# The last stage's TensorE program as a loop: rounds of sixteen tiles with fixed addresses, and a small ring for the split state

## What is computed

```python
def _L3_conv_ref(x, weight, idx_a, idx_b):
    cross = x[..., idx_a] * x[..., idx_b]
    feat = jnp.concatenate([x, x * x, cross], axis=-1)
    return jnp.einsum('bcij,cijo->bcio', feat, weight)
...
x = x + _L3_conv_ref(_gn(x), L3_conv_weight, L3_conv_idx_a, L3_conv_idx_b)
```

## Time and profile before

| | |
|---|---|
| median of 3 runs | 1283.17 us (1258.48 to 1284.13) |
| profiled execution | 1278.0 us, its span 1276.2 us, granted TensorE clock 0.677 |
| busy, share of the span | DVE 56%, PE 48%, ACT 40%, POOL 16% |
| last stage | first gather 835.8 us, last output issued 1273.8 us |
| queues | q1 (SP) 236.02 MB, q0 (POOL) 8.92 MB, q8 (instructions) 1.79 MB |
| chain that ended last | PE 31%, issue 24%, DMA 21%, DVE 18% of the span |

### The profile page before, as it was taken

How to read it: one execution, slowest core, us unless ns; L and a number is a source line. 1 busy time by engine, 2 the same in 40 slices (tenths; PEclk the granted TensorE clock), 3 DMA queues, 4 the chain that set the end, 5 groups by cost and what they waited for, 6 DMA issues and landing times.

```text
span 1276.2 us, 46246 instructions
## 1 busy us (share of the span) xinstructions
PE 607.6 (48%) x20656; PEld 484.3 (38%) x20656; DVE 713.7 (56%) x877; ACT 507.9 (40%) x716; POOL 204.3 (16%) x241
## 2 busy tenths in 40 slices
PE   2122121242699999412112122256675755556666
PEld 2112121232698989412112111034343433434344
DVE  6886565698543544796645659733453443334344
ACT  5575656570000000366555546132342333233333
POOL 1021111100111121021112110051303122121200
PEclk9555555566898989755555555687677577778777
DMA  9699999922999999789999991055657477464651
GB/s 274 157 280 226 226 230 230 237 68 59 234 235 234 231 227 240 180 230 232 212 214 218 215 309 38 8 165 172 201 187 219 159 228 218 162 201 148 217 164 55
DMA packets 50961, 246.90 MB, mean 193 GB/s; under 512 B 10992, under 2 KB 23280, under 8 KB 30256
## 3 DMA queue, kind: packets, MB, share of 16 engines
q1 hardware_dynamic: 46496, 236.02, 71.1%
q0 software_dynamic: 4336, 8.92, 2.5%
HBM read 219.20 MB, written 17.32 MB: 185 GB/s over the span
## 4 chain that ended last, share of the span: by engine, by line
PE 31%; issue 24%; DMA 21%; DVE 18%; ACT 3%; SPq 2%; POOL 1%; DVEq 0%; POOLq 0%; ACTq 0%
DMA work<-image 18%; PE psum L861 10%; PE psum L932 7%; PE psum L899 6%; PE psum L915 5%; PE psum L849 3%; DVE stats L573 2%; DVE state_b L780 2%; ACT state_b L526 2%; DMA image<-work 2%; DMA wring<-in_w 1%; DVE work L625 1%; DVE state_a L740 1%; DVE stats L744 1%; DVE state_a L618 1%
## 5 line engine op out<-in xcount | busy, mean ns | idle before, releaser
L780 DVE TENSOR_TENSOR state_b<-psum,state_b 128x512 f32<-128x512 f32 x256 | 163.8, 686 | 265.8 <-ACT state_b L526 264.6
L526 ACT ACTIVATE state_b<-psum 128x512 f32<-128x512 f32 x256 | 141.0, 596 | 292.1 <-PE psum L899 287.1
L849 PE MATMUL psum<-work,signs 96*32 96x64 f16 x6144 | 91.4, 241 | 347.8 <-DMA work<-image 307.6
L849 PEld LDWEIGHTS psum<-work,signs 96*32 96x32 f16 x6144 | 84.5, 129 | 354.8 <-issue 335.3
L861 PE MATMUL psum<-work,wring 96*128 96x128 f32 x1536 | 185.0, 285 | 37.4 <-DMA work<-image 37.4
L861 PEld LDWEIGHTS psum<-work,wring 96*128 96x128 f32 x1536 | 182.8, 201 | 39.7 <-issue 36.7
L408 ACT ACTIVATE signs<-wring 96x3072 f16<-96x3072 f32 x64 | 175.7, 2747 | 7.6 <-DMA wring<-in_w 7.6
L932 PE MATMUL psum<-state_b,wring 128*32 128x32 f32 x8192 | 125.8, 217 | 64.6 <-issue 64.1
L932 PEld LDWEIGHTS psum<-state_b,wring 128*32 128x32 f32 x8192 | 104.5, 128 | 135.6 <-issue 120.3
L682 DVE TENSOR_REDUCE abs_sums<-wring 96x2432 f32 x56 | 149.8, 2674 | 1.1
L899 PE MATMUL psum<-work,sel 64*128 64x512 f16 x512 | 108.4, 484 | 36.5 <-DMA work<-signs 17.4
(11 more groups left out here) (129 smaller groups left out, 615.9 us busy)
## 6 DMA issues: line engine op xcount, KB each, us to landing
wring<-in_w SPq DMA_DIRECT2D x96, 1152.0 KB, 16.0
wring<-in_pairs SPq DMA_DIRECT2D x64, 1024.0 KB, 5.7
work<-image SPq DMA_DIRECT2D x99, 272.0 KB, 10.7
image<-work SPq DMA_DIRECT2D x98, 128.0 KB, 4.3
work<-signs POOLq DMA_DIRECT2D x128, 64.0 KB, 5.8
state_a<-in_x SPq DMA_DIRECT2D x8, 512.0 KB, 8.6
work<-in_own SPq DMA_DIRECT2D x8, 512.0 KB, 6.5
out<-state_a SPq DMA_DIRECT2D x16, 256.0 KB, 6.0
```

Source lines behind the costliest of these rows:

```text
L526: act.activation(left[:, n % LSLOTS, :], psum[:, 2 * (n % 3), :], ACT.Copy, scale=1.0 / HALF_SCALE / HALF_SCALE).then_inc(left_made, 1)
L780: dve.tensor_tensor(feats[:, n % FSLOTS, :], psum[:, 2 * (n % 3) + 1, :], left[:, n % LSLOTS, :], ALU.mult).then_inc(feats_made, 1)
L849: last = pe.matmul(psum[g * C:(g + 1) * C, s, v * cols:(v + 1) * cols], wt[:, v, g, t, :], win[:, g * V + v + t, :], start=(v == 0 and t = ...
```

## The change

PE's last stage becomes a loop of 15 rounds, one group each, with a 16th group unrolled behind it. [...]

- `wpairs` has 4 slots instead of 6, one for each step of a group; `feats` 8 instead of 6.
- All parts of the split state lie in `parts` (each part has its own place and semaphore). POOL copies the columns of step k into slot k % 4 of a new `ring` (`copy_ring`), out of which PE gathers.
- `own_w` holds one group (256 KB and 4 x 32 KB) in one slot, and is loaded for each group; POOL copies the group's `xn` into `own_x` (`copy_own`), ACT squares it into `own_xsq`.
- `spread` moves from POOL's queue to SP's, after every eighth step.
- Own terms come in two halves, at tiles 0 and 8; a result is a half group (256 columns), added and written 32 times instead of 16.
- Gather t + 2 now waits for ACT's copy of tile t (`left_made`); the two factors use 2 and 4 banks. The mix of tile t follows each gather.
- Waits on PE compare with numbers worked out in registers.

Before, the 16 spread transfers of a part stood in POOL's queue and the own weights once a part. The diff, cut:

```diff
@@ -58,10 +58,15 @@
-WSLOTS = 6
+WSLOTS = 4
 WSTEP = PT * POS * W
-OWN = C * W
-FSLOTS = 6
+HALF = GROUP // 2
+GT = GROUP * PT
+GCOLS = GROUP * C4 * B
+OWN = GROUP * C4 * W
+ASLOTS = 2
+BSLOTS = 4
+FSLOTS = 8
...
-        xn = work[:, 0:2 * PART].rearrange("p (s n) -> p s n", s=2)
-        xsq = work[:, 2 * PART:4 * PART].rearrange("p (s n) -> p s n", s=2)
-        parts = work[:, 4 * PART:8 * PART].bitcast(F16).rearrange("p (s g n) -> p s g n", s=2, g=G)
-        own_w = work[:, STATE:STATE + 4 * OWN].rearrange("p (s k n) -> p s k n", s=2, k=2)
+        parts = work.bitcast(F16).rearrange("p (g n) -> p g n", g=G)
...
+        own_w = beside[:, 0:2 * OWN].rearrange("p (k n) -> p k n", k=2)
+        own_x, own_xsq = (beside[:, 2 * OWN + k * GCOLS:2 * OWN + (k + 1) * GCOLS] for k in range(2))
         hi_lo = signs.rearrange("p s n -> p (s n)")[:, 0:4 * PART].rearrange("p (s k n) -> p s k n", s=2, k=2)
+        ring = signs.rearrange("p s n -> p (s n)")[:, 4 * PART:4 * PART + GROUP * FCOL].rearrange("p (s n) -> p s n", s=GROUP)
...
+            load_own(0)
+            def spread(i):
+                sp.wait_ge(hi_split, i + 1)
+                sp.wait_ge(lo_split, i + 1)
+                for k in range(2):
+                    for g in range(G):
+                        for side in range(2):
+                            first = (2 * side + k) * W
+                            sp.dma_start(parts[first:first + W, g, i * PART:(i + 1) * PART],
+                                         hi_lo[g * W:(g + 1) * W, i % 2, k, :]).then_inc(parts_in[i], 16)
             for i in range(2):
-                load_own(i)
+                spread(i)
             for k in range(NK):
                 sp.wait_ge(mixed, PT * (k + 1))
                 if k + WSLOTS < NK:
                     load_pairs(k + WSLOTS)
-                if k % KPART == 1 and 2 <= k // KPART + 1 < V:
-                    sp.wait_ge(own_used, k // KPART * (KPART // GROUP))
-                    load_own(k // KPART + 1)
-                if k % GROUP == 1 and k > GROUP:
-                    sp.wait_ge(result_made, k // GROUP)
-                    cols = slice((k // GROUP - 1) * GROUP * C4 * B, k // GROUP * GROUP * C4 * B)
+                grp, half = k // GROUP, k % GROUP // HALF
+                if k % GROUP == 1 and grp + 1 < NGROUP:
+                    sp.wait_ge(own_used, 2 * (grp + 1))
+                    load_own(grp + 1)
+                if k % (2 * GROUP) == 2 * GROUP - 1 and (grp + 3) // 2 < V:
+                    spread((grp + 3) // 2)
+                if k % HALF == 1 and k > HALF:
...
+            def copy_ring(k):
+                if k % (2 * GROUP) == 0:
+                    pool.wait_ge(parts_in[k // GROUP // 2], 16 * 4 * G)
+                if k >= GROUP:
+                    pool.wait_ge(gathered, (k - GROUP + 1) * PT)
+                pool.tensor_copy(ring[:, k % GROUP, :].rearrange("p (g n) -> p g n", g=G),
+                                 parts[:, :, k * C4 * B:(k + 1) * C4 * B]).then_inc(ring_made, 1)
+            def copy_own(grp):
+                pool.wait_ge(xn_made[3], grp // 2 + 1)
+                if grp:
+                    pool.wait_ge(own_used, 2 * grp)
+                pool.tensor_copy(own_x, xn[:, grp // 2 % 2, grp % 2 * GCOLS:(grp % 2 + 1) * GCOLS]).then_inc(own_copied, 1)
+            m_op, r_op = (t[:, 0:B].unsqueeze(1).to_broadcast([P, C, B]) for t in (mean, rstd))
...
+            normalise(1)
+            for grp in range(NGROUP):
+                copy_ring(grp * GROUP)
+                copy_ring(grp * GROUP + 1)
+                copy_own(grp)
+                if grp % 2 and grp // 2 + 2 < V:
+                    normalise(grp // 2 + 2)
+                copy_ring(grp * GROUP + 2)
+                copy_ring(grp * GROUP + 3)
         CONSTS = 16 * 5
...
+            def gather(j, t):
+                if t % PT == 0:
+                    pe.wait_ge(ring_made, j * GROUP + (t // PT + 1))
                 for side in range(2):
                     half = slice(side * 2 * W, (side + 1) * 2 * W)
-                    last = pe.matmul(psum[:, 2 * (n % 3) + side, :], sel[half, t * P:(t + 1) * P],
-                                     parts[half, i % 2, :, cq * C4 * B:(cq + 1) * C4 * B], start=True, stop=True)
+                    bank = (0, ASLOTS)[side] + t % (ASLOTS, BSLOTS)[side]
+                    last = pe.matmul(psum[:, bank, :], sel[half, t % PT * P:(t % PT + 1) * P],
+                                     ring[half, t // PT, :], start=True, stop=True)
                 last.then_inc(gathered, 1)
-            def own_terms(grp):
-                i, first = grp // (KPART // GROUP), grp % (KPART // GROUP) * GROUP * C4
-                if grp >= 2:
-                    pe.wait_ge(result_made, grp - 1)
-                if first == 0:
-                    pe.wait_ge(own_in[i % 2], 16 * (1 + G) * (i // 2 + 1))
-                    pe.wait_ge(squared, i + 1)
+            def own_terms(half):
                 for k in range(2):
-                    for c in range(first, first + GROUP * C4):
+                    for c in range(HALF * C4):
+                        n = half * HALF * C4 + c
                         for g in range(G):
                             q = slice(g * W, (g + 1) * W)
-                            last = pe.matmul(psum[q, 6 + grp % 2, (c - first) * B:(c - first + 1) * B],
-                                             own_w[q, i % 2, k, c * W:(c + 1) * W], (xn, xsq)[k][q, i % 2, c * B:(c + 1) * B],
-                                             start=(k == 0 and c == first), stop=False, skip_group_check=True)
+                            last = pe.matmul(psum[q, 6 + half, c * B:(c + 1) * B], own_w[q, k, n * W:(n + 1) * W],
+                                             (own_x, own_xsq)[k][q, n * B:(n + 1) * B],
+                                             start=(k == 0 and c == 0), stop=False, skip_group_check=True)
                 last.then_inc(own_used, 1)
...
+            def mix(j, t):
+                s = t // PT
+                if t % PT == 0:
+                    pe.wait_ge(pairs_in[s], j * 16 + 16)
...
-                for m in range(n, n + 2):
-                    mix(m)
+            def group(j, ahead):
+                for t in range(GT):
+                    if t == 0:
+                        pe.wait_ge(own_in, j * (16 * (1 + G)) + 16 * (1 + G))
+                        pe.wait_ge(own_copied, j + 1)
+                        pe.wait_ge(squared, j + 1)
+                    if t % (GT // 2) == 0:
+                        pe.wait_ge(result_made, j * 2 + (t // (GT // 2) + 1))
+                    if t + ASLOTS < GT or ahead:
+                        pe.wait_ge(left_made, j * GT + (t + 1))
+                        if t + ASLOTS < GT:
+                            gather(j, t + ASLOTS)
+                        else:
+                            gather(j + 1, t + ASLOTS - GT)
+                    if t % (GT // 2) == 0:
+                        own_terms(t // (GT // 2))
+                    mix(j, t)
+            for t in range(ASLOTS):
+                gather(0, t)
+            with pe.Fori(0, NGROUP - 1) as j:
+                group(j, True)
+            group(NGROUP - 1, False)
```

More of the change, by code:

```diff
@@ L351, in _ @@
             pool.wait_ge(conv_done, 3 * U)
[L352 to L359, removed]
-                if i >= 2:
[L361 to L374, removed]
+            pool.wait_ge(signs_made, 2 * U)
+            pool.wait_ge(abs_made, 2 * U)
+            pool.memset(own_w[:, 1, :], 0.0).then_inc(own_zeroed, 1)
+            def copy_ring(k):
[5 more added lines that the diff above has]
+                                 parts[:, :, k * C4 * B:(k + 1) * C4 * B]).then_inc(ring_made, 1)
@@ new lines, in copy_own, with normalise @@
+            def copy_own(grp):
[4 more added lines that the diff above has]
+            m_op, r_op = (t[:, 0:B].unsqueeze(1).to_broadcast([P, C, B]) for t in (mean, rstd))
+            def normalise(i):
+                if i >= 2:
+                    pool.wait_ge(squared, 2 * (i - 1))
@@ L507, in _, with high, square_own @@
             take_root(rstd[:, 0:B], tmp_a[:, 0:B], 6)
-            def high_and_square(i):
+            def high(i):
                 act.wait_ge(xn_made[3], i + 1)
                 if i >= 2:
-                    act.wait_ge(parts_in[i % 2], 16 * 4 * G * (i // 2))
+                    act.wait_ge(parts_in[i - 2], 16 * 4 * G)
                 act.activation(hi_lo[:, i % 2, 0, :], xn[:, i % 2, :], ACT.Copy, scale=HALF_SCALE).then_inc(hi_split, 1)
[L515 to L519, removed]
-            for n in range(TILES):
-                if n % (KPART * PT) == KPART * PT // 4 and n // (KPART * PT) + 1 < V:
-                    high_and_square(n // (KPART * PT) + 1)
+            def square_own(grp):
+                act.wait_ge(xn_made[3], grp // 2 + 1)
+                if grp:
+                    act.wait_ge(own_used, 2 * grp)
```

(33 more changed lines are left out.)

74 lines of the change are left out of this document (37 added, 37 removed).

## The result

The changed kernel takes 1162.34 us (median of 4, 1155.42 to 1167.35) against 1275.78 us: ratio 0.9196, 95% interval 0.9091 to 0.9301. The forecast was 1142 us in a range of 1102 to 1200. The direction, the size and the mechanism of the gain held; what bounds the loop afterwards was not what I had forecast. The gain is 113 us where 141 were forecast from the base of 1283.17 us.

The account below looks back on a forecast made before the run. PE's instruction fetch was taken to bound the last stage. Cutting 14 groups from 28.0 to 18.0 us saves 140; 1276.2 - 140 + 1.5 = 1137.7 us span, 1139.5 profiled, 1142 as median; range 1102 to 1200.

Parts of the forecast that it names:

- The fetch bounds the stage: Last stage: PE's unrolled program runs at the pace of instruction fetch, 28.0 us a group, 4.5 us per 256-instruction line.
- The body is kept, over seven lines: PE's new loop: its 1631 instructions cover seven lines, which stay in instruction memory across rounds without being fetched again.
- PE's pace, 15.4 us at full clock: Loop group on PE with its handshake: 8 x 1.59 + 2.7 = 15.4 us at full clock, 19.7 at half.
- Register arithmetic, 0 to 2 us a group: PE's loop: some 20 register operations a group between matmuls, 0 to 0.1 us each, 0 to 2 us in all.
- DMA, 17.9 us: Loop group's transfers: 5.37 MB at 300 GB/s take 17.9 us, with 14.6 and 20.8 as ends.
- T = 18 us: Loop's group period, the slower middle of PE and DMA: 18 us, ends 15.4 to 20.8; saves 140 us over 14 groups.
- SP "at most 20 of 36 us", with three steps of slack: SP's queue: issuing for two groups takes at most 20 of 36 us; pair loads behind the spread's 8 us have slack.
- rival 1: Own weights in one slot land up to 5 us late: 22 us a group, 1198 us; 15 in 100 together with rival 2.
- Three copies, +1.5 us: Start of the last stage: two ring copies and the own copy, less gathers running meanwhile, add 1.5 us (1 to 3).
- POOL hidden: POOL's copies and half a normalise, 5 to 8 us a group, are hidden because copies are asked for three steps ahead.
- Rival 3: PE's loop keeps no lines: each round fetches seven, 34.7 us a group, 1376 us (1330 if the branch is free); 11 in 100.
- Rival 2: PE's loop loses one line each round, a 3.3 us gap: 21.5 us a group, 1191 us; 15 in 100 with rival 1.

Follow-up runs that it names:

- The last kernel: Against the changed kernel, the spread is issued by POOL from part 2 on and own weights are loaded in two halves: 1122.73 us, ratio 0.8837.

## Why the prediction was right, point by point

- **The fetch bounds the stage**: shown. It goes from 99 packets to 12 in the last stage, "issue" of PE from 140.3 to about 16 us; written out again, 135.8 us of it come back.
- **The body is kept, over seven lines**: shown, and the count was exact enough that 40 more instructions changed nothing and 100 did. One figure of the argument was wrong: I set the two packets of the earlier trace rows against 24, but that stretch holds 1813 matmuls, 4.7 of the 8 rounds, so it is two against some 14. The conclusion stands.
- **PE's pace, 15.4 us at full clock**: 14.3. The new order is a little faster at full clock than the old one (0.74 against 0.80 us a tile, out of 7.16 less 1.25 us of own terms), so the handshake that I kept from the earlier trace rows was an upper bound. At half clock it is slower: a tile takes 1.13 us in the first group (854.49 to 855.62) against 0.99. That the gather and the mix alternate twice as often may be the reason; it is not shown. In group 0 it is part of the 4.5 us that I had put at 0.
- **Register arithmetic, 0 to 2 us a group**: 0 as far as the traces show. The kernel written out has none, and its mixes follow each other at the same 0.71 and 0.78 us at full clock (936.19, 936.90, 937.68) as those of the loop (862.13, 862.84, 863.62), and at 1.13 us at half.
- **DMA, 17.9 us**: too dear. The last kernel moves a group in 16.1 us at a share of 0.96. The three stretches of the earlier trace rows were full because a burst had queued, with spread transfers among them, not because 300 GB/s is all they carry.
- **T = 18 us**: 19.0 measured, the right size for the wrong reason. I had put DMA bandwidth there; what stands there is PE's 14.3 us and the late own weights. That the number came out near 18 is luck.
- **SP "at most 20 of 36 us", with three steps of slack**: this is the step that failed. The sum over two groups was right, and I checked the block of the spread against the pair loads, which have three steps. The own weights stand in the same queue and have eight tiles, under 8 us. I had named that lead in rival 1 and expected pair *data* ahead of them, up to 5 us late in every group. They were 5.8 to 7.6 us late in every second group: in the stretch shown, the *issuing* of the spread held them back by 2.9 us and bunched pair loads ahead of them, which made their landing 3.6 us longer. So the data that I named had a part, but only behind that block; with the block on POOL's queue 19.5 of the 40.9 us stayed. The issue of one spread transfer, 0.66 us, was also dearer than the 0.53 of the earlier trace rows.
- **Three copies, +1.5 us**: +3.8 from `spread` to the first own terms. One copy is 0.61 us, inside the bounds of the earlier trace rows; the rest is the dearer issue (16 x 0.16 = 2.6 us against POOL's 0.50).
- **POOL hidden**: right in the changed kernel, whose ring copies never kept PE waiting once the stage ran.
- **Rival 3, nothing is kept**: its mechanism exists, but not for seven lines. Nine lines show it at 4.1 us a line, where I had 4.5 and 3.3 for the branch. Rival 2 (one line lost each round, 3.3 us) does not exist as I priced it: in the two runs over eight lines a round with a fetch fetched them all.

## What to carry to other kernels

When an engine's idle time ends in "issue" at equal distances of instructions, count the instructions between the stalls: a long unrolled stretch runs at the pace of the fetch, here 4.5 us for 256 instructions, and a loop whose body fits, with the line behind it, takes that away. Then count from the start of the program where the body lies, since 100 to 130 instructions ahead of it cost 21 and 92 us here, of the 126 that the loop had gained. When transfers move to another queue, list for each of them what stands behind it and how long that can wait; here the one with the shortest lead decided, not the sum.

## What the runs showed of the hardware

- A loop of 1631 instructions on PE runs with no fetch at all over 14 rounds (no q8 packet from 871 to 1137 us with 20 matmuls ahead). Over nine lines every line is fetched in every round (9 to 11 packets a group).
- In between, over eight lines, rounds are either free or fetched whole, and how many are fetched differs: one cluster of nine packets with 100 instructions ahead, six with 130 (one run each).
- The transfer engines of the core carried 327 GB/s over 225 us at a share of 0.96; the three convolutions of the kernel before, at a share of 0.97 to 1.02, carry 225 to 240 GB/s (66 to 186, 330 to 430 and 550 to 700 us), so GB/s at a full share is no constant of the engines.
- After each wait of 5.8 to 7.6 us in the changed kernel PE ran its next own terms at the lower clock (1.93 us for 128 against 1.29; granted 0.53 from 898.6 to 902). With those waits gone the granted clock of the loop rose from 0.90 to 0.97.
